# Experts' second products from rounded rows and exact rests: squares on ScalarE, gates and rounding on GpSimd, rests on VectorE

## The reference

```python
def mlp(x, wfc, wproj):
    return jnp.square(jax.nn.relu(x @ wfc)) @ wproj
shared = mlp(x, w_fc_sh, w_proj_sh)
scores = sigmoid(xf @ router_w.T)
_, idx = top_k(scores + balance_bias, 2)
combine = ...                                   # 8 gates a token, two of them not zero, of sum 1
h = jnp.square(jax.nn.relu(jnp.einsum('nc,ech->neh', xf, w1)))
y = jnp.einsum('neh,ehc->nec', h, w2)
out = h_in + shared + jnp.einsum('nec,ne->nc', y, combine)      # xf: layernorm of h_in
```

## Time and profile before

| | us |
|---|---|
| median of 3 runs | 4240.48 (4234.64 to 4243.27) |
| the profiled execution | 4242.51 |
| its span, first to last instruction | 4240.8 |
| mean granted clock of PE over the span | 0.979 |

### The profile page before, as it was taken

The page is one execution under the profiler, slowest core; times in us unless marked ns, Lnnn a source line. Parts: engine busy times, 40 slices in busy tenths (PEclk is TensorE's granted clock), DMA queues, the critical chain, the costliest instruction groups (busy, mean ns, idle before and its releaser), DMA issues. The chain is left out here.

```text
span 4240.8 us, 84769 instructions
## 1 busy us (share of the span) xinstructions
PE 4025.1 (95%) x28203; PEld 3938.8 (93%) x28203; DVE 2885.2 (68%) x7468; ACT 2497.5 (59%) x6686; POOL 1280.7 (30%) x1423
## 2 busy tenths in 40 slices
PE   4986799999999999999999999999999799999999
PEld 4886699999999999999999999999999799999999
DVE  4675566766666766676766676667666677777776
ACT  2554666666766666666676666666665344444443
POOL 1323322232232232223223223222222344444443
PEclk8998899999999999999999999999999899999999
DMA  8641100000000000000000000000000322222222
GB/s 188 141 114 48 36 1 1 1 25 1 2 24 2 1 2 24 1 1 24 1 1 25 1 1 2 24 1 1 13 1 1 92 93 93 93 91 87 82 90 90
DMA packets 88974, 161.67 MB, mean 38 GB/s; under 512 B 5706, under 2 KB 75937, under 8 KB 85055
## 3 DMA queue, kind: packets, MB, share of 16 engines
q1 hardware_dynamic: 85118, 152.66, 12.6%
q0 software_dynamic: 944, 2.42, 0.3%
q10 hardware_dynamic: 2576, 2.36, 0.2%
HBM read 127.82 MB, written 29.60 MB: 37 GB/s over the span
## 5 line engine op out<-in xcount | busy, mean ns | idle before, releaser
L637 POOL TENSOR_TENSOR att_prob<-att_prob,att_total 99x396 f32<-99x396 f32 x768 | 649.9, 846 | 2108.7 <-DVE att_total L869 2108.7
L877 DVE TENSOR_REDUCE att_npeak<-att_s 99x2 f32<-99x396 f32 x768 | 434.8, 566 | 449.4 <-PE att_s L1090 440.5
L718 ACT ACTIVATE att_probT<-att_t 99x396 f32<-99x396 f32 x768 | 384.1, 500 | 572.1 <-PE att_t L1056 566.7
L730 ACT ACTIVATE att_prob<-att_s,att_npeak 99x198 f32<-99x198 f32 x1536 | 636.6, 424 | 137.3 <-DVE att_npeak L877 135.4
L1073 PE MATMUL att_o<-att_probT,att_vx 99*96 99x198 f32 (+1 forms) x3072 | 653.5, 335 | 1.1 <-DVE att_rx L862 1.1
L1090 PE MATMUL att_s<-att_kx,att_qx 96*99 96x198 f32 (+1 forms) x3072 | 642.5, 332 | 5.2 <-DVE att_qx L821 2.2
L1278 POOL TENSOR_TENSOR ffn_hidden<-ffn_relu 128x384 f32<-128x384 f32 x462 | 425.3, 927 | 482.6 <-ACT ffn_relu L1307 480.6
L1090 PEld LDWEIGHTS att_s<-att_kx,att_qx 96*99 96x99 f32 (+1 forms) x3072 | 481.4, 166 | 12.4 <-issue 6.0
L1307 ACT ACTIVATE ffn_relu<-ffn_h 128x384 f32<-128x384 f32 x462 | 225.7, 489 | 448.4 <-PE ffn_h L1527 446.5
L1539 PE MATMUL ffn_y<-ffn_down,ffn_hidden 128*128 128x192 f32 x2772 | 487.3, 327 | 1.6 <-DVE ffn_hidden L1431 1.6
L1073 PEld LDWEIGHTS att_o<-att_probT,att_vx 99*96 99x96 f32 (+1 forms) x3072 | 469.5, 179 | 4.4 <-issue 1.4
(11 more groups left out here) (241 smaller groups left out, 8117.8 us busy)
## 6 DMA issues: line engine op xcount, KB each, us to landing
ffn_gates<-gate_rows SPq DMA_DIRECT2D x66, 768.0 KB, 5.5
tok_pixels<-in_x SPq DMA_DIRECT2D x24, 1568.0 KB
ffn_hid<-hidden SPq DMA_DIRECT2D x35, 288.0 KB, 3.0
att_xres<-hidden SPq DMA_DIRECT2D x8, 1188.0 KB
hidden<-att_xres SPq DMA_DIRECT2D x8, 1188.0 KB
ffn_acc<-hidden SPq DMA_DIRECT2D x33, 288.0 KB, 2.9
out_hidden<-ffn_acc SPq DMA_DIRECT2D x33, 288.0 KB, 2.4
hidden<-tok_rows SPq DMA_DIRECT2D x7, 1176.0 KB
```

The source lines that it names most:

```text
L637: nc.gpsimd.tensor_tensor(prob[:, i % 2, :, :], prob[:, i % 2, :, :], view(total[:, i % 2, :], [[1, 2], [0, NTOK]]), ALU.mult).then_inc(pr ...
L718: nc.scalar.activation(probT[:, i % 2, :], t_bank[0:HALF, 0:2 * NTOK], ACT.Copy).then_inc(probT_made, 1)
L730: ins = nc.scalar.activation(prob[:, i % 2, h, :], s_bank[i % 2][0:HALF, h * NTOK:(h + 1) * NTOK], ACT.Exp, bias=npeak[:, i % 2, h:h + 1], ...
L877: nc.vector.tensor_reduce(npeak[:, i % 2, :], s_bank[i % 2][0:HALF, 0:2 * NTOK].rearrange("p (h k) -> p h k", h=2), AX.X, ALU.max, negate= ...
```

## The change

The second products are no longer made in fp32. Each chunk of hidden rows is split into `hh`, rounded to fp32r, and `hl`, the exact rest; the weights `down` are split once in the same manner. For each tile PE makes two fp32r products: `hh` with both halves of the weights side by side (384 columns), and `hl` with the rounded half (192 columns). The product of the two rests is left out. `sums` adds two halves of each bank.

The work moves. ACT squares what it has rectified. POOL multiplies by the gates (whole chunks, from a `gates` tile that now has one 384-column row for each of the 12 gated chunks, loaded by eight DMAs of SP instead of two) and rounds into `hh`: 11 times a block as a copy, three times as an addition of zeros. DVE subtracts to get `hl`, two chunks ahead of PE (LEAD). `hh` and `hl` have seven slots (SPLITS); `chunk_done` tells when one is free. PE waits for `split_made`. Before the loop PE waits for the split weights.

```diff
-        down = m.sb("down", [128, HT, DIM])
+        raw_down = m.sb("raw_down", [128, HT, DIM])
+        down = m.sb("down", [128, HT, 2, DIM], fp32r)
+        hh, hl = m.sb("hh", [128, SPLITS, BT], fp32r), m.sb("hl", [128, SPLITS, BT], fp32r)
...
-        gates = m.sb("gates", [128, 2, EXPERTS, BT])
+        gates = m.sb("gates", [128, 2, HT - 2, BT])
...
+                sp.sem_inc(chunk_done, HT - 1)
...
-                        half = EXPERTS // 2
-                        src = gate_rows[s, half * h:half * (h + 1), :]
-                        sp.dma_start(gates[:, s, half * h:half * (h + 1), :],
-                                     bass.AP(tensor=src.tensor, offset=src.offset, ap=[[0, 128], [BT, half], [1, BT]])
-                                     ).then_inc(gates_in[s][h], 16)
+                        for c, lo, hi, first in ((0, 0, 128, 0), (2, 0, 128, 1), (1, 0, 64, 0), (1, 64, 128, 1)):
+                            src = gate_rows[s, 4 * h + first, :]
+                            sp.dma_start(view(gates[lo:hi, s, 6 * h + c, :], [[3 * BT, 2], [1, BT]]),
+                                         bass.AP(tensor=src.tensor, offset=src.offset, ap=[[0, hi - lo], [2 * BT, 2], [1, BT]])
+                                         ).then_inc(gates_in[s][h], 16)
...
-                def squares(k, s):
-                    for n, j in enumerate(CHUNKS):
-                        rows = 64 if j == 13 else 128
-                        pool.wait_ge(relu_made, k * HT + n + 1)
-                        nc.gpsimd.tensor_tensor(hidden[0:rows, s, j, :], relu[0:rows, (n + 2 * s) % 4, :], relu[0:rows, (n + 2 * s) % 4, :], ALU.mult
-                                                ).then_inc(squared, 1)
-
-                squares(0, 0)
+                def gate_chunk(k, pair, s, n):
+
+                    if n in (SHARED, SHARED + GATED // 2):
+                        pool.wait_ge(gates_in[s][0 if n == SHARED else 1], pair * 64 + 64)
+                    pool.wait_ge(squared, k * HT + n + 1)
+                    j = CHUNKS[n]
+                    nc.gpsimd.tensor_tensor(hidden[:, s, j, :], hidden[:, s, j, :], gates[:, s, j, :], ALU.mult).then_inc(gated, 1)
+
+                def high_may(k, n):
+
+                    if n < SHARED:
+                        pool.wait_ge(squared, k * HT + n + 1)
+                    else:
+                        pool.wait_ge(gated, k * GATED + n - SHARED + 1)
+                    if n == SPLITS - 1:
+                        pool.wait_ge(down_done, k * TB)
+                    else:
+                        pool.wait_ge(chunk_done, k * (HT - 1) + n + SPLITS + (0 if n >= SPLITS else 1))
+
+                def split_high(k, s, n):
+                    nc.gpsimd.tensor_copy(hh[:, n % SPLITS, :], hidden[:, s, CHUNKS[n], :]).then_inc(hh_made, 1)
+
+                def split_high_alone(k, s, n):
+                    high_may(k, n)
+                    nc.gpsimd.tensor_tensor(hh[:, n % SPLITS, :], hidden[:, s, CHUNKS[n], :], zeros[:, :], ALU.add).then_inc(hh_made, 1)
+
+                def block_of(k, pair, s, more):
+                    gate_chunk(k, pair, s, SHARED)
+                    for n in range(HT):
+                        if n + LEAD + 1 < HT:
+                            high_may(k, n + LEAD)
+                            gate_chunk(k, pair, s, n + LEAD + 1)
+                            split_high(k, s, n + LEAD)
+                        elif n + LEAD < HT:
+                            split_high_alone(k, s, n + LEAD)
+                        elif more:
+                            split_high_alone(k + 1, 1 - s, n + LEAD - HT)
+
+                nc.gpsimd.memset(zeros[:, :], 0.0).then_inc(down_cleared, 1)
+                pool.wait_ge(down_cleared, 3)
+                for n in range(LEAD):
+                    split_high_alone(0, 0, n)
                 with pool.Fori(0, (BLOCKS - 1) // 2) as pair:
                     for s in range(2):
-                        squares(pair * 2 + s + 1, 1 - s)
+                        block_of(pair * 2 + s, pair, s, True)
+                block_of(BLOCKS - 1, BLOCKS // 2, 0, False)
...
                 def relu_of(k, s, n):
+                    act.wait_ge(up_done, k * HT + n + 1)
                     rows = 64 if CHUNKS[n] == 13 else 128
-                    act.wait_ge(up_done, k * HT + n + 1)
                     if n >= 4 or not isinstance(k, int):
                         act.wait_ge(squared, k * HT + n - 3)
+                    nc.scalar.activation(relu[0:rows, n % 2, (n // 2 + s) % 2, :], h_bank[n % 2][0:rows, 0:BT], ACT.Relu).then_inc(relu_made, 1)
                     if CHUNKS[n] == 13:
                         if not isinstance(k, int):
                             act.wait_ge(routed, k)
-                        nc.scalar.activation(odds[0:EXPERTS, :], h_bank[n % 2][64:64 + EXPERTS, 0:BT], ACT.Copy)
-                    nc.scalar.activation(relu[0:rows, (n + 2 * s) % 4, :], h_bank[n % 2][0:rows, 0:BT], ACT.Relu).then_inc(relu_made, 1)
-                    if CHUNKS[n] == 13:
-                        act.wait_ge(relu_made, k * HT + n + 1)
+                        nc.scalar.activation(odds[0:EXPERTS, :], h_bank[1][64:64 + EXPERTS, 0:BT], ACT.Copy).then_inc(odds_made, 1)
+                        act.wait_ge(odds_made, k + 1)
                         nc.scalar.activation(odds[0:EXPERTS, :], odds[0:EXPERTS, :], ACT.Exp, scale=-1.0).then_inc(expo_made, 1)
+
+                def square(k, s, n):
+                    rows = 64 if CHUNKS[n] == 13 else 128
+                    act.wait_ge(relu_made, k * HT + n + 1)
+                    nc.scalar.activation(hidden[0:rows, s, CHUNKS[n], :], relu[0:rows, n % 2, (n // 2 + s) % 2, :], ACT.Square
+                                         ).then_inc(squared, 1)
...
+                act.wait_ge(w_in, 16 * WEIGHTS)
+                nc.scalar.activation(down[:, :, 0, :], raw_down[:, :, :], ACT.Copy).then_inc(down_high, 1)
...
                             relu_of(it + 1, 1 - s, n)
+                            square(it + 1, 1 - s, n)
...
-                def gate_hidden(it, pair, s, n):
-
-                    j = CHUNKS[n]
-                    i, c = j // 3, j % 3
-                    if n == SHARED or n == SHARED + GATED // 2:
-                        h = 0 if n == SHARED else 1
-                        dve.wait_ge(gates_in[s][h], pair * 16 + 16)
-                    dve.wait_ge(squared, it * HT + n + 1)
-                    halves = {0: ((0, 128, 2 * i),), 1: ((0, 64, 2 * i), (64, 128, 2 * i + 1)), 2: ((0, 128, 2 * i + 1),)}[c]
-                    for lo, hi, e in halves:
-                        ins = nc.vector.tensor_tensor(hidden[lo:hi, s, j, :], hidden[lo:hi, s, j, :], gates[lo:hi, s, e, :], ALU.mult)
-                    ins.then_inc(gated, 1)
+                def rest(k, s, n):
+
+                    dve.wait_ge(hh_made, k * HT + n + 1)
+                    nc.vector.tensor_tensor(hl[:, n % SPLITS, :], hidden[:, s, CHUNKS[n], :], hh[:, n % SPLITS, :].bitcast(fp32), ALU.subtract
+                                            ).then_inc(split_made, 1)
 
                 def sums(it, pair, s):
 
                     dve.wait_ge(acc_in[s], pair * 16 + 16)
                     for t in range(TB):
                         dve.wait_ge(down_done, it * TB + t + 1)
-                        nc.vector.tensor_tensor(acc[:, s, t, :], y_bank[t][:, 0:DIM], acc[:, s, t, :], ALU.add).then_inc(summed, 1)
+                        nc.vector.tensor_tensor(acc[:, s, t, :], y_bank[t][:, 0:DIM], acc[:, s, t, :], ALU.add).then_inc(half_summed, 1)
+                    for t in range(TB):
+                        dve.wait_ge(half_summed, it * TB + t + 1)
+                        nc.vector.tensor_tensor(acc[:, s, t, :], y_bank[t][:, DIM:2 * DIM], acc[:, s, t, :], ALU.add).then_inc(summed, 1)
...
+                dve.wait_ge(down_high, 1)
+                nc.vector.tensor_tensor(down[:, :, 1, :], raw_down[:, :, :], down[:, :, 0, :].bitcast(fp32), ALU.subtract
+                                        ).then_inc(down_low, 1)
+                for n in range(LEAD):
+                    rest(0, 0, n)
                 K_BODY = first_steps.n - 2
                 with dve.Fori(0, (BLOCKS - 1) // 2) as pair:
                     for s in range(2):
                         it = pair * 2 + s
                         st = Steps(dve, dve_step, first_steps.n + it * K_BODY)
-                        for n in range(SHARED, SHARED + AHEAD):
-                            gate_hidden(it, pair, s, n)
                         for n in range(HT):
-                            if SHARED <= n and n + AHEAD < HT:
-                                gate_hidden(it, pair, s, n + AHEAD)
+                            if n + LEAD < HT:
+                                rest(it, s, n + LEAD)
+                            else:
+                                rest(it + 1, 1 - s, n + LEAD - HT)
...
+                    if n == 3:
+                        pe.wait_ge(odds_made, k + 1)
...
```

(13 more changed lines are left out.)

27 lines of the change are left out of this document (17 added, 10 removed).

## The result

The changed kernel took 4549.6 us (median of four runs, 4546.5 to 4552.8) beside 4241.0 of the kernel before: a ratio of 1.0732, with a 95% interval of 1.0716 to 1.0748. Its profiled execution took 4549.95 (span 4548.1). The forecast was 4290, range 4200 to 4345: the sign is right, the size is far off and outside the range.

A forecast was written before the change was run, and what follows sets the result against it. PE bounds the kernel before; after the change the gates' loop through POOL and DVE would, at 28.6 us a block. 4242.5 + 36 (loop) + 5 (ahead) + 7 (behind) = 4290.5, forecast 4290, range 4200 to 4345.

The forecast's parts named there:

- PE's part: Second products on PE: the fp32r pair costs 0.29 us instead of 0.327, saving 1.55 us a block.
- (c): Rival for PE's short fp32r product: it streams as fp32, 34.8 us a block, about 4490; (b), (c) and table loads 0.09.
- (d): Rival for PE's second products: pair stays at 0.327, nothing else binds, 4255 us; no chance of its own given.
- ACT hides the squares: ACT gains 14 squares, +6.9 us a block, 19 busy of 26 to 28, costed at nothing; extra table loads improbable.
- the lock: POOL and DVE: each POOL operation, copies included, holds DVE its whole length; 4255 to 4345 us, chance 0.56.
- Rival (a): POOL and DVE: copies leave DVE alone, PE's 25.9 us a block rules, 4205 us; with milder mixtures below 4232, 0.28.
- rival (b): POOL's copy costs as much as its two-input operation: 32.7 us a block, 4421 us; (b), (c) and table loads 0.09.
- the walk to the gate value: POOL and DVE from the gates' landing to the block's last gate value: 17.5 + 9 x 0.29 + 0.8, 20.9 us.
- What follows is fixed: From last gate value to next block's gates (turn, ACT copy, store, loads): a fixed 7.8 us, 6.8 before plus 1.
- Two more issues: SP's gate loads: two more issues of 0.4 us and half as many bytes again add 1 us (0.5 to 2).
- 5 forecast: Ahead of the loop, PE waits for the weights' split by ACT and DVE: 5 us.
- 7 forecast: Behind the loop, nothing covers POOL's last work: 22 us in all against PE's former tail, +7 us.

The follow-up runs named there:

- Experiment 5: Kernel before with only its down products changed to the two fp32r products, reading one fixed hh and hl, hidden rows left out: 4188.4 us.
- Experiment 8: Kernel before with only its squares moved from POOL to ACT: 4239.0 us over eight runs, ratio 1.0004.
- experiment 7: Changed kernel with each of POOL's 11 copies a block made a second time into a buffer nothing reads: 4570.3 us.
- Experiment 1: Changed kernel with ACT's square root for the next block moved behind its copy of the turned gates: 4470.5 us.
- Experiment 2: Changed kernel with two gate loads a block instead of eight, some chunks multiplied by another expert's gates: 4451.2 us.
- experiment 6: Changed kernel with gate products back on DVE, POOL only rounding, root behind the copy, four loads from gates stored three times: 4310.8 us, ratio 1.0174.
- experiment 11: Experiment 10 with the kernel before's gates tile, two loads and 16 gate operations, and the root behind the copy: 4296.6 us, ratio 1.0143.
- experiment 10: Changed kernel with the gate products back on DVE and POOL only rounding, its eight loads and ACT order kept: 4314.1 us.
- experiment 12: Experiment 11 with the routing, and the turn and copy of the gates, two chunks earlier: 4326.4 us, ratio 1.0213.
- experiment 9: Changed kernel with root behind the copy, routing two chunks earlier and two plain loads, some chunks using another expert's gates: 4401.9 us.

## Why the prediction was right in sign and wrong in size

**Right: what bounded, and PE's part.** Experiment 5 saved 1.6 us a block where 1.55 was forecast. PE's timeline of the changed kernel at full clock:
```profile
4040.61 0.36 PE L1593 MATMUL ffn_y<-ffn_down,ffn_hh 128*128 128x384 f32 x1
4040.81 0.25 PE L1594 MATMUL ffn_y<-ffn_down,ffn_hl 128*128 128x192 f32 x1
4040.89 0.36 PE L1593 MATMUL ffn_y<-ffn_down,ffn_hh 128*128 128x384 f32 x1
...
4041.75 0.36 PE L1593 MATMUL ffn_y<-ffn_down,ffn_hh 128*128 128x384 f32 x1
```
Four pairs in 4041.75 - 4040.61 = 1.14, 0.285 each, where 0.29 was forecast. The estimate worked out from the Trainium skill (TensorE: Matmul & The Clock Gate, Back-to-back issue gap), 0.26, was too low. The page gives that formula for an isolated product and says that it under-counts short ones that load weights; the 0.285 of this pair agrees with that. Rivals (c) and (d) fall with these rows.

**Right: ACT hides the squares.** Experiment 8 shows it. The table loads stayed at 63 for the 32 bodies in both kernels and in experiment 8, so Square cost none.

**Right: the lock, and that copies are part of it.** The rows of L1477 and L1459 show it. Rival (a), in which copies leave DVE alone, falls. So does rival (b), in which a copy costs as much as a two-input operation: it took 0.50, and 0.83 only where a rest got in ahead of it; that its 32.7 a block and 4421 us lay nearer to the measured 36.6 and 4549.6 than the forecast is chance. The Trainium skill (GPSIMD Engine Reference, Key points) had excepted no GpSimd instruction, and this case agrees: 0.41 instead of 0.18 beside a copy of 0.51.

**Nearly right: the walk to the gate value**, 20.9 forecast and 23.3 measured. POOL ran dry 22.4 us after the landing, 2.3 later than the 20.1 of the forecast, and the last steps took 1.0 instead of 0.8. The earlier trace rows showed a product of a tile with itself; one of two tiles lasts 0.18 more (1.01) and starts 0.96 ahead of the next operation (4012.00 to 4012.96, where the copy starts), 0.13 more than the 0.83 that the sum used. Fifteen such operations, the additions among them, are 2.0 of the 2.3; the first product stood 0.25 alone. The copies start 0.46 ahead of what follows, as forecast, and eight holds of 0.33 cost what nine of 0.29 were to cost. By experiment 7 the argument itself, POOL's sum of work, was only half right all the same: eleven more operations did not move the gate value. That it came out near is in part luck; it seems to be so because the number of POOL's operations and of the places that DVE's steps need are nearly equal here.

**Wrong: "What follows is fixed".** This is the step that failed. The tail was 7.8 in the forecast and 13.3 to 13.5 in the trace, and it was not fixed, for two reasons above all:
- The copy on ACT. Before, the root had run 2 us ahead of the copy and was done in time; ACT's timeline of the kernel before:
```profile
3830.27 0.30 ACT L1290 ACTIVATE ffn_sd<-ffn_mv,ffn_eps 128x3 f32<-128x3 f32 x1
...
3832.58 0.48 ACT L1316 ACTIVATE ffn_gateT<-ffn_r 8x384 f32<-8x384 f32 x1
```
PE's turn had started at 3831.97, so its copy ended 1.1 behind it. With the routing late, the statistics behind it on DVE were late as well, and the copy stood behind them on another engine: 3.7 us from turn to copy's end instead of 1.1. The prediction named the statistics and the root as standing behind the routing, but charged them to nobody. Experiment 1 prices it at 2.5.
- The loads. "Two more issues" and half as many bytes were costed at 1. Four loads stand where one stood, so three more issues lie ahead of the first half's last, not two. All eight are issued in 4.61 us, each in 0.4 to 0.6; the fourth is issued at 4038.22, 1.6 behind the first, and landed at 4044.24, 6.0 after its issue. Over all of them the view of the tile ffn_gates gives:
```profile
DMA to landing us min/median/max: 3.4/5.9/9.1
```
1.6 + 6.0 and 0.15 to the start are the 7.7 of the walk; before, the first half was one load that landed after 4.4. Experiment 2 prices eight loads against two at 3.0.

So the tail is longer than its 7.8 by 5.7: 0.6 from the gate value to the turn, since the 6.8 that it was built on began at the turn; 2.6 for the copy; and 2.5 for store and loads (9.2 behind the copy's end, instead of 6.8 - 1.1 + 1 = 6.7). The two experiments bear out the larger two: 2.5 for the root, and 3.0 for the loads, of which the forecast had charged 1. With the 2.4 of the walk that is 8.1 a block above the 28.6 forecast, against the 8.0 measured. The span is divided thus: 292.4 up to the last turn (32 bodies of 9.1), with nothing ahead of the loop (5 forecast); 4 in the last tail, where the gates land at 4520.7, 12 behind the last turn, instead of at 4224.0, 8 behind it; and 11 behind the last landing, 27.4 instead of 16.8 (7 forecast; twelve gate products that take 0.13 more each are 1.6 of the difference, the rest was not followed up).

**A knock-on that had no term.** PE that waits is also granted less. PE's timeline of the changed kernel:
```profile
4028.19 0.69 PE L1593 MATMUL ffn_y<-ffn_down,ffn_hh 128*128 128x384 f32 x1 [2.04 <-DVE ffn_hl L1477]
4028.67 0.36 PE L1594 MATMUL ffn_y<-ffn_down,ffn_hl 128*128 128x192 f32 x1
4028.83 0.57 PE L1593 MATMUL ffn_y<-ffn_down,ffn_hh 128*128 128x384 f32 x1
4029.20 0.36 PE L1594 MATMUL ffn_y<-ffn_down,ffn_hl 128*128 128x192 f32 x1
4029.36 0.57 PE L1593 MATMUL ffn_y<-ffn_down,ffn_hh 128*128 128x384 f32 x1
```
After idle times of 1.23 and 2.04 us the pairs come 0.53 apart instead of 0.285: the lower of the clock's two levels, 1.2 instead of 2.4 GHz. The mean of the stretch is 0.90. It reaches into the loop: the turn took 0.84 (4031.55 to 4032.39) instead of 0.49. How much of the loss this makes was not measured by itself. In experiments 6 and 11 the stretch has 1.00 again, with PE idle for 58 and 60 of 800 us, so it follows from the waits and not from the product. The sum of idle time does not tell it: experiments 10 and 12, with 57 and 62 us idle, have 0.97 and 0.96.

**The root of it.** No single step had to be slow. In experiment 10 copy and loads are as bad as in the changed kernel (4 us from turn to copy, 7.3 from load issue to the next block), and 235 of 309 us are gone, since the gate value comes 7.4 earlier (15.9 for 23.3). The gate products on POOL close the loop, and each microsecond in the tail counts only while it is closed. Mending the rest would not have made this division of work pay: experiment 9, with the gate products still on POOL but the routing, the copy and the loads mended, needs 32.0. Nor would giving the gate products back: experiment 11 then stands at 28.8, bound by DVE, a rival that the prediction did not have. Both lie above the 27.4 of before. Where DVE's work would stand in the changed kernel with its loop open was not measured.

## What to carry to other kernels

Work moved to GpSimd costs VectorE too: count the VectorE steps in the stretch that combine two SBUF tiles (and TENSOR_SCALARs on one) and charge each one a whole running GpSimd operation, however short the step, instead of comparing busy times; the reductions, reciprocals and sums from PSUM of this loop were not held. When a change delays a step, follow everything behind it on its own engine to whoever waits for that on others; here the statistics behind the routing held a root, and the root held a copy on which the next block hung. A tail that is called fixed must be walked row by row, with each DMA's issue and landing.
